# LoRA folds in pairs: the factor stack held in both partition halves, two 64-row products at a time

## What is computed

```
h1 = xn @ (w1 + 2 * B1 A1).T        h3 = xn @ (w3 + 2 * B3 A3).T
g  = silu((silu(h1) * h3) @ (w2 + 2 * B2 A2).T)
```

## Time and profile before

| | us |
|---|---|
| median of three runs | 411.89 |
| the profiled execution | 412.15 |
| its span, first to last instruction | 410.4 |
| TensorE matmul busy | 405.3 |
| VectorE busy | 164.9 |
| ScalarE busy | 107.1 |
| GpSimd busy | 66.8 |

### The profile page before, as it was taken

One profiled execution on the slowest core, in us unless ns is written; L12 is line 12 of the kernel. 1 busy time (PEld: TensorE's weight loads), 2 busy tenths in 40 slices (PEclk: granted clock), 3 DMA queues, 4 the chain that ended last, 5 costly groups with the idle time before them and its releaser, 6 DMA issues.

```text
span 410.4 us, 5012 instructions
## 1 busy us (share of the span) xinstructions
PE 405.3 (99%) x1860; PEld 338.6 (83%) x1860; DVE 164.9 (40%) x259; ACT 107.1 (26%) x176; POOL 66.8 (16%) x130
## 2 busy tenths in 40 slices
PE   8999999999999999999999999999999999999996
PEld 8988888888888888888888888888888888888885
DVE  5777775654693321232244222132334212211125
ACT  7554333322441111122221111212222111111122
POOL 6227627330700114000000101400000000000000
PEclk9999999999999999999999999999999999999999
DMA  8663943220516101000006101000002000000002
GB/s 274 161 218 101 306 133 80 82 90 20 153 52 206 51 2 52 2 0 0 0 29 215 66 0 52 0 0 0 0 0 102 2 0 0 2 0 0 2 0 102
DMA packets 14338, 26.20 MB, mean 64 GB/s; under 512 B 2560, under 2 KB 4608, under 8 KB 14320
## 3 DMA queue, kind: packets, MB, share of 16 engines
q1 hardware_dynamic: 13872, 24.85, 18.9%
q0 software_dynamic: 160, 0.59, 0.4%
q10 hardware_dynamic: 288, 0.52, 0.3%
HBM read 20.33 MB, written 4.53 MB: 61 GB/s over the span
## 4 chain that ended last, share of the span: by engine, by line
PE 91%; DVE 4%; DMA 2%; issue 1%; ACT 1%; SPq 0%; POOL 0%; DVEq 0%; POOLq 0%
PE h L936 19%; PE h L935 19%; PE h L934 19%; PE f L935 10%; PE f L934 10%; PE f L936 10%; PE h L957 2%; DMA trig_sb<-trig_dram 2%; PE h L965 1%; PE spare L921 1%; DVE raw L732 1%; DVE w L747 1%; PE spare L936 1%; PE spare L935 1%; PE spare L934 1%
## 5 line engine op out<-in xcount | busy, mean ns | idle before, releaser
L934 PE MATMUL h<-xt,w 128*128 (+2 forms) x340 | 131.5, 387 | 0.0
L935 PE MATMUL h<-xt,w 128*128 (+2 forms) x340 | 131.1, 386 | 0.0
L936 PE MATMUL h<-xt,w 128*128 (+2 forms) x340 | 131.1, 386 | 0.0
L936 PEld LDWEIGHTS h<-xt,w 128*128 128x128 f32 x340 | 63.9, 188 | 12.8
L935 PEld LDWEIGHTS h<-xt,w 128*128 128x128 f32 x340 | 63.9, 188 | 12.7
L934 PEld LDWEIGHTS h<-xt,w 128*128 128x128 f32 x340 | 63.9, 188 | 12.6
L796 DVE TENSOR_TENSOR g<-g,h 128x512 f32<-128x512 f32 x40 | 27.5, 688 | 111.1 <-PE h L936 110.9
L801 DVE TENSOR_TENSOR ghl<-g,ghl 128x512 fp32r<-128x512 f32 x44 | 31.6, 719 | 92.5 <-ACT ghl L625 92.5
L934 PE MATMUL f<-ghl,w2f 128*128 128x512 f32 x176 | 68.6, 390 | 0.0
L625 ACT CAST ghl<-g 128x512 fp32r<-128x512 f32 x44 | 27.3, 621 | 157.9 <-PE f L936 144.7
L935 PE MATMUL f<-ghl,w2f 128*128 128x512 f32 x176 | 68.6, 389 | 0.0
(11 more groups left out here) (131 smaller groups left out, 306.2 us busy)
## 6 DMA issues: line engine op xcount, KB each, us to landing
raw<-w_dram SPq DMA_DIRECT2D x28, 256.0 KB, 3.4
xres<-xT_dram SPq DMA_DIRECT2D x4, 1024.0 KB, 7.2
outT_dram<-xres SPq DMA_DIRECT2D x15, 256.0 KB, 2.4
rows_next<-x_dram SPq DMA_DIRECT2D x4, 512.0 KB, 3.6
scale_rows<-scales_scratch SPq DMA_DIRECT2D x3, 512.0 KB, 4.1
rows<-x_dram SPq DMA_DIRECT2D x2, 512.0 KB, 6.8
raw<-w_dram SPq DMA_DIRECT2D x4, 224.0 KB, 2.4
lora_stack<-lora_spread_split SPq DMA_DIRECT2D x3, 204.0 KB, 3.7
```

The costliest lines, as they stand in the source:

```text
L934: pe.matmul(out, w[1], m[0], start=start, stop=False)
L935: pe.matmul(out, w[0], m[1], start=False, stop=False)
L936: return pe.matmul(out, w[0], m[0], start=False, stop=stop)
```

## The change

The stack now lies twice in `lst`: each rank has four partitions in place of eight, once in partitions 0 to 63 (copied by SyncE's queue as before) and once in 64 to 127 (six more DMAs, issued by GpSimd on its own queue behind `small_ready`). Ten pairs of folds are issued together: each fold of a pair reads one half of the partitions and writes its own spare bank, their matmuls taken in turns. The two folds at j=1 "gate" read the lower half alone. Folds that stay single read all 128 partitions, so their product is doubled, and VectorE's factor is halved. In place of one fold behind the gate product and one behind the up product, j=3 to 8 have a pair behind the gate product; at j=2 two pairs stand behind gate and up.

```diff
+HALF_STEP = STACK_STEP // 2
+LOWER, UPPER = slice(0, P // 2), slice(P // 2, P)
@@ def folds(place, j)
     if j == 2:
-        return {"gate": [(1, 4)], "up": [(3, 3), (3, 4)], "down": [(2, 2)]}[place]
+        return {"gate": [(1, 4), (3, 3)], "up": [(3, 4), (2, 2)], "down": []}[place]
     if place == "down":
         return [(2, j)] if j < HT - 2 else [(2, HT - 2), (2, HT - 1)]
-    return [(1 if place == "gate" else 3, j + 2)] if j < HT - 2 else []
+    return [(1, j + 2), (3, j + 2)] if place == "gate" and j < HT - 2 else []
+BEFORE_COPY = folds("gate", 1)
+PAIRS = [folds("up", 1), folds("gate", 2), folds("up", 2)] + [folds("gate", j) for j in range(3, HT - 2)] + [folds("down", HT - 2)]
+PAIRED = [f for pair in PAIRS for f in pair]
+def fold_scale(kind, j):
+    return LORA_SCALE if j <= PLAIN[kind] or (kind, j) in BEFORE_COPY + PAIRED else LORA_SCALE / 2
@@ sync
-                    sync.dma_start(lst[n:P:STACK_STEP, cols].bitcast(F32).rearrange("r (k c) -> r k c", k=P // R),
+                    sync.dma_start(lst[n:P // 2:HALF_STEP, cols].bitcast(F32).rearrange("r (k c) -> r k c", k=P // R),
@@ vector, fold_add
-                dve.wait_ge(fold_ready, n + 1)
+                dve.wait_ge(fold_ready, max(FOLD_NO[f_] for f_ in pair_of(kind, j)) + 1)
-                                               scalar=LORA_SCALE, in1=rt, op0=ALU.mult, op1=ALU.add) \
+                                               scalar=fold_scale(kind, j), in1=rt, op0=ALU.mult, op1=ALU.add) \
@@ tensor
+            def fold_pair(one, other):
+                if one == PAIRED[0]:
+                    pe.wait_ge(copy_in, 2 * len(STACK) * 16)
+                banks = [take(0, ("fold", f_), True) for f_ in (one, other)]
+                parts = [fold_parts(*f_) for f_ in (one, other)]
+                for n in range(max(parts)):
+                    for f_, bankt, count, rows in zip((one, other), banks, parts, (LOWER, UPPER)):
+                        if n < count:
+                            mm = fold_part(bankt, *f_, n, rows)
+                        if n == count - 1:
+                            mm.then_inc(fold_ready, 1)
@@ gpsimd, behind small_ready
+            pool.wait_ge(spread_lo, 1)
+            pool.wait_ge(stack_cleared, 2)
+            for n, (st, mv) in enumerate(STACK):
+                for hl, cols, lane_cols in (...):
+                    pool.dma_start(lst[P // 2 + n:P:HALF_STEP, cols].bitcast(F32).rearrange("r (k c) -> r k c", k=P // R),
+                                   spread_hl[:, hl, lane_cols].bitcast(F32)).then_inc(copy_in, 16)
```

More of the change, by code:

```diff
@@ L157, in folds, with pair_of @@
     if j == 2:
-        return {"gate": [(1, 4)], "up": [(3, 3), (3, 4)], "down": [(2, 2)]}[place]
+        return {"gate": [(1, 4), (3, 3)], "up": [(3, 4), (2, 2)], "down": []}[place]
     if place == "down":
         return [(2, j)] if j < HT - 2 else [(2, HT - 2), (2, HT - 1)]
-    return [(1 if place == "gate" else 3, j + 2)] if j < HT - 2 else []
+    return [(1, j + 2), (3, j + 2)] if place == "gate" and j < HT - 2 else []
 FOLDS = FOLD_FIRST + [f for j in range(HT) for p in ("gate", "up", "down") for f in folds(p, j)]
 FOLD_NO = {f: n for n, f in enumerate(FOLDS)}
+BEFORE_COPY = folds("gate", 1)
+PAIRS = [folds("up", 1), folds("gate", 2), folds("up", 2)] + [folds("gate", j) for j in range(3, HT - 2)] + [folds("down", HT - 2)]
+PAIRED = [f for pair in PAIRS for f in pair]
+def pair_of(kind, j):
+    return next((pair for pair in PAIRS if (kind, j) in pair), [(kind, j)])
+def fold_scale(kind, j):
+    return LORA_SCALE if j <= PLAIN[kind] or (kind, j) in BEFORE_COPY + PAIRED else LORA_SCALE / 2
 POOL_LO = [(1, 3), (3, 3), (3, 4)]
@@ L347, in build @@
         spread_in, stack_in, stack_cleared = sem("spread_in"), sem("stack_in"), sem("stack_cleared")
+        copy_in = sem("copy_in")
         s4_in, trig_in, bvec_in, dft_in = sem("s4_in"), sem("trig_in"), sem("bvec_in"), sem("dft_in")
@@ L906, in take, with fold_parts, fold_part @@
                 return sp[bk]
-            def fold(kind, j):
-                bankt = take(0, ("fold", (kind, j)), True)
+            def fold_parts(kind, j):
+                return 1 if kind == 2 else len(part_chunks(j))
+            def fold_part(bankt, kind, j, n, rows):
                 plain = j <= PLAIN[kind]
@@ L912, in fold @@
                 fac = lr if plain else lst
-                if (kind, j) == FOLDS[len(FOLD_FIRST)]:
-                    pe.wait_ge(stack_in, 2 * len(STACK) * 16)
[L915 to L922, removed]
-                mm.then_inc(fold_ready, 1)
+                if kind == 2:
+                    return pe.matmul(bankt[0:hs(j), :], fac[rows, a + j * P:a + j * P + hs(j)], fac[rows, bc:bc + D],
+                                     start=True, stop=True)
+                t0, units = group(j)
+                c = part_chunks(j)[n]
+                return pe.matmul(bankt[:, n * units:(n + 1) * units], fac[rows, a + c * P:a + (c + 1) * P],
+                                 fac[rows, bc + t0 * P:bc + t0 * P + units], start=True, stop=True)
+            def fold(kind, j):
+                bankt = take(0, ("fold", (kind, j)), True)
+                if (kind, j) == BEFORE_COPY[0]:
+                    pe.wait_ge(stack_in, 2 * len(STACK) * 16)
+                for n in range(fold_parts(kind, j)):
+                    mm = fold_part(bankt, kind, j, n, LOWER if (kind, j) in BEFORE_COPY else slice(0, P))
+                mm.then_inc(fold_ready, 1)
+            def fold_pair(one, other):
[9 more added lines that the diff above has]
+                            mm.then_inc(fold_ready, 1)
             def turn_rows(r):
@@ L1045, in extras @@
             def extras(j, place):
-                for kind, t in folds(place, j):
-                    fold(kind, t)
+                if folds(place, j) in PAIRS:
+                    fold_pair(*folds(place, j))
+                else:
+                    for kind, t in folds(place, j):
+                        fold(kind, t)
                 if (j, place) == KAPPA_AT:
@@ L1198, in _ @@
             pool.sem_inc(small_ready, 1)
+            pool.wait_ge(spread_lo, 1)
+            pool.wait_ge(stack_cleared, 2)
+            for n, (st, mv) in enumerate(STACK):
+                for hl, cols, lane_cols in ((st, slice(0, ST_COLS), slice(0, LANES_ST)),
+                                            (mv, slice(ST_COLS, LORA_COLS), slice(LANES_ST, LANES_ST + LANES_MV))):
+                    pool.dma_start(lst[P // 2 + n:P:HALF_STEP, cols].bitcast(F32).rearrange("r (k c) -> r k c", k=P // R),
+                                   spread_hl[:, hl, lane_cols].bitcast(F32)).then_inc(copy_in, 16)
             pool.wait_ge(den_ready, 3)
```

## The result

The changed kernel takes 420.19 us (median of six, 419.02 to 422.54) against 411.78 for the kernel before on the same chip: ratio 1.0206, 95% interval 1.0191 to 1.0221. The forecast was 416.2 with a range to 420.0. The sign was right, the size was not: +8.4 us, not +4.3. The profiled execution is the quickest of the six, 419.02 us with a span of 417.2.

A forecast was written before the change was run, and what follows sets the result against it. TensorE's stream was taken to bound the kernel, busy 405.3 of 410.4 us. The terms 0.5 + 0.8 + 1.5 + 1.5 = +4.3 us, added to the median 411.89, gave 416.2 us, slower; range 411.4 to 420.0.

The forecast's parts named there:

- The array's 64-row products: Pairs at j=3, 4, 6, 7, 8 lose 0.11 us each, the final one gains 0.03; together +0.5, ends -1.4 and +4.1.
- a plain pair: Two folds issued together where nothing else changes: 0.39 + 0.2 = 0.59 us in place of 0.48.
- the weight loads: Four per pair of kinds 1 and 3, passing one by one at 0.0975 us each: 0.39 us.
- a change: Array going from 128 to 64 rows or back, 22 times: 0.1 us each taken, bounds 0 and 0.34.
- the last pair: Folds (2,9) and (2,10), with two weight loads: from 0.47 to 0.44 us.
- The wait at j=2: Pairs behind gate and up wait for banks VectorE has yet to read; net +0.8 us.
- the second wait: Pair behind up at j=2 waits for the bank of (3,3), starting at 35.75 us.
- Kappa: It takes the bank (1,7) has just filled, so TensorE waits for VectorE's add: net +1.5 us, between +1.0 and +2.3.
- The six added DMAs: Their transfers beside SyncE's delay trig_sb, then ScalarE, VectorE and the bank of (2,1): +1.5 us, from options 0, 1.5, 3.0.
- The clock: Granted clock falling below 1.00 behind a wait would make the prediction wrong; the trace of before had no case.
- Rival B: Mode drain decides: each array change costs 0.34 us and nothing overlaps, giving 420.7 us; chance 0.17.

The follow-up runs named there:

- the run with the late copies: Changed kernel with GpSimd's copies held until trig_sb landed, folds at j=1 and j=2 single on the lower half, pairs only from j=3: 416.06 us.

## Why the prediction was wrong in size

- **The array's 64-row products, forecast +0.5: right in kind, some 0.9 in size.** Overlap complete (0.23 saved), two changes 0.39, so a plain pair costs 0.62, close to the forecast 0.59. That is luck in part, as two errors cancel: the weight loads, priced at 0.39 for four, do not show, since a pair with two loads takes as long as one with four; and a change costs twice the 0.1 taken. For the last pair they do not cancel: it was forecast at 0.44 and costs 0.62 too. Six pairs at 0.15 each are 0.9. The Trainium skill's page "TensorEngine Tiling (Array Packing)", Tiling Modes, says that a change of mode drains the engine; the 0.195 for a change in the run with the late copies, inside the bounds of 0 and 0.34, agrees, though no row shows the drain itself. The Trainium skill's page "TensorE: Matmul & The Clock Gate", Part 3, says that tiles of a pack take little more than one; the equal 1.08 us for one fold and for two agrees.
- **The wait at j=2, forecast +0.8: +0.64, but by one wait in place of two.** From the down product of j=1 to the gate product of j=3 the shift grows from 29.74 - 25.58 = 4.16 to 4.80. The pair behind the gate product waits as forecast; the second wait, ahead of the pair behind the up product, is not there.
- **Kappa, forecast +1.5: there.** From 5.14 to 6.28, +1.14; kappa started 1.61 behind the pair's start, forecast 1.98 (60.74 - 58.76).
- **The six added DMAs, forecast +1.5 by way of trig_sb: this step failed.** trig_sb's delay was sized well, 1.34, but the forecast said of TensorE that it "did not wait for them at 21.49" and went on to the next transfer. That no wait shows in the trace of before was read as a margin. SyncE's six share the same engines in the same microseconds, so the work worked out for trig_sb, 3.0 us, had first to be put on the stack's own last DMA, which TensorE needs sooner. With the 20.7 of the trace of before that gives a landing at 23.7; measured is 23.72. The wait was 2.34 us, a shift of 2.37. So the estimate of the copies' work agrees here; it was put on the wrong transfer, and the margin of 0.8 us was not looked up.
- **The clock, in no term.** It was named as what would make the forecast wrong. In the profiled execution the product behind the wait for the stack took 1.63 longer, of which some 0.2 are, as an estimate, the changes of the array at its two ends (0.1 each, as at the undisturbed pair). Span times (1 - mean clock) is 1.7, 3.8, 1.7, 2.1, 5.5 and 3.8 us for the six executions, and the span less that is 415.2 to 416.0 in all of them: nearly the whole spread of the changed kernel is the clock. Behind which of the two waits it fell is seen in the profiled execution alone. For the kernel before the same product is 0.4 in the profiled execution and at most 0.8 in the others.

On the profiled pair of executions the measured terms are 2.37 (stack) + 1.63 (clock) + 0.25 (the first two folds, on 64 rows, 24.73 - 23.86 against 0.62) + 0.64 (j=2) + 1.14 (kappa) = 6.03 of the 6.8. The rest is 0.34 from j=3 to j=5 (5.14 - 4.80) and 0.51 from (2,5) to (2,9), both stretches with pairs, less 0.09 for the pair (3,2), (1,3) (29.74 - 29.15 = 0.59 in place of 0.68). Rival B's 420.7 is close to the measured time, but not for its reason: a change costs 0.195 and not 0.34, and the halves overlap.

Not settled: how long the clock stays down. It differs between executions of one program, and the runs show only that it falls behind these waits in some executions, and in none of the four where the one is filled and the other gone. No version beat the kernel before; the one nearest to it has the new places and none of the second stack.

## What to carry to other kernels

An operation that shows no wait may still have no margin: before adding transfers to a stretch where the DMA engines are busy, ask for each landing in that stretch, the nearest in time first, which engine needs it and how late it may come. Halves of the array do run side by side, but going there and back must be paid from what the overlap saves: here 0.39 us against 0.23 per pair, so a pair alone among full products loses, whatever else is right. From these two figures two pairs one behind the other should just pay, 0.46 against 0.39; that is an estimate, and no run tried it. When operations are moved, walk the ring of buffers again: kappa's wait came only from taking another bank.

## What the runs showed of the hardware that was not expected

- A 64-row matmul of 512 columns costs the same by itself and with a second one on the other half (1.08 us from the full product ahead to the second one behind, in both cases), and going from 128 to 64 rows and back adds 0.39 us to the stream, once for a stay.
- TensorE's granted clock fell to the lower level behind a wait of 2.34 us in the changed kernel's profile, and in some executions behind kappa's wait of 1.11 us and its eight small matmuls, for 1.6 us of lost time; behind waits of 1.24 and 1.79 us without such small matmuls it did not in the profiled executions.
- One DMA of 1416 KB within SBUF, beside 2 MB of loads of rows and residual, took 18.2 us to land.
